# One bank of scores in eight copied by ScalarE, its maximum kept by VectorE from bf16 copies

## The reference, cut to what matters

```python
q = (query @ Wq.T + bq).reshape(b, -1, 16, 16)      # 256 latent tokens
k = (key @ Wk.T + bk).reshape(b, -1, 16, 16)        # 4096 context tokens
v = (value @ Wv.T + bv).reshape(b, -1, 16, 16)
attn = softmax(einsum('bqhd,bkhd->bhqk', q, k) / sqrt(16))
out = einsum('bhqk,bkhd->bqhd', attn, v) ; out @ Wo.T + bo
```

## Time and profile before

| | us |
|---|---|
| median of 3 runs | 3688.89 (3686.14 to 3690.83) |
| span of the profiled execution, first to last instruction | 3677.2 |
| outside the span: median less span | 11.7 |
| DVE busy in the whole span | 2126.4 (58%) |
| ACT busy in the whole span | 1525.3 (41%) |

### The profile page before, as it was taken

How to read it: one execution, slowest core, us unless ns; L and a number is a source line. 1 busy time by engine, 2 the same in 40 slices (tenths; PEclk the granted TensorE clock), 3 DMA queues, 4 the chain that set the end, 5 groups by cost and what they waited for, 6 DMA issues and landing times. The chain is left out here.

```text
span 3677.2 us, 56678 instructions
## 1 busy us (share of the span) xinstructions
PE 3396.7 (92%) x22589; PEld 2130.7 (58%) x22608; DVE 2126.4 (58%) x3378; ACT 1525.3 (41%) x2294; POOL 904.2 (25%) x665
## 2 busy tenths in 40 slices
PE   8989898999999999999967888999988889999899
PEld 5855695655656556565634576444455644445575
DVE  4335313555555555555468621999855279995654
ACT  2335211424334243343355522466745137665621
POOL 1032001426345163452517512000011120000430
PEclk9999999999999999999988999999999989999999
DMA  5358562000000100000097533756500386550010
GB/s 190 105 188 273 186 249 84 7 6 5 7 1 1 61 7 9 4 4 1 12 241 281 206 143 120 190 117 121 101 26 24 124 226 125 117 106 22 1 48 36
DMA packets 228860, 346.91 MB, mean 94 GB/s; under 512 B 104176, under 2 KB 177584, under 8 KB 223984
## 3 DMA queue, kind: packets, MB, share of 16 engines
q1 hardware_dynamic: 228208, 342.16, 32.1%
q0 software_dynamic: 384, 1.05, 0.1%
HBM read 257.15 MB, written 86.02 MB: 93 GB/s over the span
## 5 line engine op out<-in xcount | busy, mean ns | idle before, releaser
L1421 POOL TENSOR_TENSOR L1x_acc<-L1x_acc,L1x_pr 128x512 f32<-128x512 f32 x256 | 418.0, 1633 | 135.7 <-ACT L1x_pr L1605 117.4
L1605 ACT ACTIVATE L1x_pr<-L1x_pss 128x1024 f32<-128x1024 f32 x272 | 278.4, 1024 | 288.2 <-PE L1x_pss L1515 280.5
L1651 DVE TENSOR_TENSOR L1x_acc<-L1x_acc,L1x_pr 128x512 f32<-128x512 f32 x256 | 255.4, 997 | 213.2 <-ACT L1x_pr L1605 209.4
L1234 DVE TENSOR_REDUCE L3x_pk<-L3x_psm 128x1 f32<-128x512 f32 x512 | 328.8, 685 | 25.9 <-PE L3x_psm L1063 19.4
L1234 DVE TENSOR_REDUCE L2x_pk<-L2x_psm 128x1 f32<-128x512 f32 x512 | 328.8, 685 | 20.7 <-PE L2x_psm L1063 14.1
L1211 ACT ACTIVATE L3x_pr<-L3x_pss 128x1024 f32<-128x1024 f32 x256 | 248.1, 1021 | 106.3 <-PE L3x_pss L1106 106.0
L1211 ACT ACTIVATE L2x_pr<-L2x_pss 128x1024 f32<-128x1024 f32 x256 | 248.1, 1021 | 102.0 <-PE L2x_pss L1106 101.8
L1629 DVE TENSOR_REDUCE L1x_pk<-L1x_psm 128x2 f32<-128x1024 f32 x144 | 168.0, 1167 | 211.1 <-PE L1x_psm L1453 211.1
L1515 PE MATMUL L1x_pss<-L1x_Q,L1x_K 64*128 64x256 f32 x2176 | 279.3, 376 | 0.0
L1479 PE MATMUL L1x_pss<-L1x_w,L1x_cT 128*128 128x256 f32 x1088 | 257.5, 387 | 0.0
L1474 PE MATMUL L1x_pss<-L1x_cT,L1x_w 128*128 128x512 f32 (+1 forms) x576 | 256.4, 584 | 0.5 <-DMA L1x_cT<-normed_context 0.5
(11 more groups left out here) (742 smaller groups left out, 6126.7 us busy)
## 6 DMA issues: line engine op xcount, KB each, us to landing
f0e_wt<-in_f_pieces SPq DMA_DIRECT2D x10, 3072.0 KB, 11.5
offset_rows<-s_rows SPq DMA_DIRECT2D x32, 768.0 KB, 5.8
L2x_KS<-L2x_key_parts SPq DMA_DIRECT2D x24, 1024.0 KB, 12.8
L3x_KS<-L3x_key_parts SPq DMA_DIRECT2D x24, 1024.0 KB, 12.8
s_add<-offset_rows SPq DMA_DIRECT2D x32, 512.0 KB, 7.5
n_cT<-in_ctxT SPq DMA_DIRECT2D x32, 512.0 KB, 4.6
f1e_wt<-in_f_pieces SPq DMA_DIRECT2D x8, 2048.0 KB, 12.7
L2x_key_parts<-n_kst SPq DMA_DIRECT2D x32, 384.0 KB, 2.8
```

The source lines that it names most:

```text
L1234: nc.vector.reduce_max(pk[:, n % 2, h * QT + qt, j:j + 1], psm[:, x % 3, :], AX).then_inc(turn_read, 1)
L1421: i = nc.gpsimd.tensor_tensor(acc[:, n, 1, :, :], acc[:, n, 1, :, :], pr[:, A % RING, :, 1, :], ALU.add)
L1605: nc.scalar.activation(pr[:, A % RING, :, :, :].rearrange("p h e q -> p (h e q)"), pss[:, x:x + 2, :].rearrange("p h n -> p (h n)"), ACT.E ...
L1651: i = nc.vector.tensor_tensor(acc[:, n, 0, :, :], acc[:, n, 0, :, :], pr[:, A % RING, :, 0, :], ALU.add)
```

## The change

In every unit from 1 on, the products i = 7, 15, ..., 55 (the second of their pair, all of query tile 1 of the group's last head, key chunks 0 to 6) are no longer read by DVE from PSUM. ACT copies the bank to SBUF as bf16 (into `most` for i = 7, into one of two buffers `side` for the others), and DVE takes the elementwise maximum of `most` and the copy. Number 63 is still read as before. When it is read, DVE reduces the 7 other columns of `mx`, then `most` (128 x 512 bf16) to one column, waits for that, and makes the last column of `mx` by a third reduce over two numbers. The copies stand in ACT's queue behind the second exponential of a pair of slots. PE's `claim` waits for whichever engine reads the bank. The buffers lie in `qp`, which is not used in the loop.

```diff
+    ASIDE = NJ - 1
+        side, most = qp[:, 0, :, :], qp[:, 1, :, :]
+        def beside(n, i):
+            return n >= 1 and i % 8 == 7 and i // 8 < ASIDE
+        def beside_before(n, i):
+            return ASIDE * (n - 1) + i // 8
...
-            def claim():
+            def claim(side_copy=None):
                 x = taken[0]
                 taken[0] += 1
                 if x >= 3:
-                    pe.wait_ge(turn_read, x - 2)
+                    pe.wait_ge(*readers[x - 3])
+                if side_copy is None:
+                    by_dve[0] += 1
+                readers.append((turn_read, by_dve[0]) if side_copy is None else (aside, side_copy + 1))
                 return x
...
+            def copy_beside(n, first, last):
+                for i in range(first, last):
+                    if beside(n, i):
+                        c = beside_before(n, i)
+                        act.wait_ge(turn, turns[n, i] + 1)
+                        if i < 8 and n >= 3:
+                            act.wait_ge(peak, n - 1)
+                        elif i >= 24:
+                            act.wait_ge(aside_read, c - n - 1)
+                        into = most[:, n % 2, :] if i < 8 else side[:, c % 2, :]
+                        nc.scalar.copy(into, psm[:, turns[n, i] % 3, :]).then_inc(aside, 1)
+            act.wait_ge(scratch_out, 16 * KC)
+            act.wait_ge(sel_mm, 2 * NU)
+            copy_beside(1, 0, AHEAD)
             for a in range(UNITS * STEPS):
...
+                if a % 2:
+                    for x in (a % STEPS - 1, a % STEPS):
+                        copy_beside(*of_slot(a // STEPS, x))
...
             def read_peaks(n, first, last):
                 for i in range(first, last):
                     x = written()
+                    if beside(n, i):
+                        c = beside_before(n, i)
+                        if i >= 8:
+                            dve.wait_ge(aside, c + 1)
+                            if i >= 16:
+                                dve.wait_ge(aside_read, c - n)
+                            nc.vector.tensor_tensor(most[:, n % 2, :], most[:, n % 2, :], side[:, c % 2, :], ALU.max).then_inc(aside_read, 1)
+                        continue
                     nc.vector.reduce_max(pk[:, n % 2, h * QT + qt, j:j + 1], psm[:, x % 3, :], AX).then_inc(turn_read, 1)
...
+                    elif i == NP - 1:
+                        dve.wait_ge(turn_read, reads[0])
+                        nc.vector.reduce_max(mx[:, n % 2, 0:UH * QT - 1], pk[:, n % 2, 0:UH * QT - 1, :], AX)
+                        dve.wait_ge(aside_read, (ASIDE - 1) * n)
+                        link(nc.vector.reduce_max(pk[:, n % 2, UH * QT - 1, 0:1], most[:, n % 2, :], AX))
+                        nc.vector.reduce_max(mx[:, n % 2, UH * QT - 1:UH * QT], pk[:, n % 2, UH * QT - 1, 0::NJ - 1], AX).then_inc(peak, 1)
```

More of the change, by code:

```diff
@@ L922, in narrow_attention @@
     ONE = len(KPART) * hd
+    ASIDE = NJ - 1
     names = ("w_here wv_here q_mm q_act part1 part2 sel_mm sel_in masked masked_more scratch_out qs_in kh_in0 kh_in1 ks_in0 ks_in1 v_in0 v_in1 cleared ones_rows ones_in "
-             "c_here0 c_here1 c_here2 c_here3 v_mm v_ev v_out0 v_out1 v_out2 turn turn_read peak scored exps averaged o_copied chain").split()
+             "c_here0 c_here1 c_here2 c_here3 v_mm v_ev v_out0 v_out1 v_out2 turn turn_read aside aside_read peak scored exps averaged o_copied chain").split()
     with Tensors(nc) as u, stage(nc, *[pre + "_" + n for n in names]) as (block, *sems):
         (w_here, wv_here, q_mm, q_act, part1, part2, sel_mm, sel_in, masked, masked_more, scratch_out, qs_in, kh_in0, kh_in1, ks_in0, ks_in1, v_in0, v_in1, cleared,
-         ones_rows, ones_in, c_here0, c_here1, c_here2, c_here3, v_mm, v_ev, v_out0, v_out1, v_out2, turn, turn_read, peak, scored, exps, averaged, o_copied, chain) = sems
+         ones_rows, ones_in, c_here0, c_here1, c_here2, c_here3, v_mm, v_ev, v_out0, v_out1, v_out2, turn, turn_read, aside, aside_read, peak, scored, exps, averaged, o_copied, chain) = sems
         kh_in, ks_in, v_in, c_here, v_outs = (kh_in0, kh_in1), (ks_in0, ks_in1), (v_in0, v_in1), (c_here0, c_here1, c_here2, c_here3), (v_out0, v_out1, v_out2)
@@ L966, in of_slot @@
             return (m, i, i + NP // SLOTS) if m < UNITS else (m, 0, 0)
+        def beside(n, i):
+            return n >= 1 and i % 8 == 7 and i // 8 < ASIDE
+        turns = {}
+        def beside_before(n, i):
+            return ASIDE * (n - 1) + i // 8
         @block.sync
@@ L1040, in _ @@
             taken = [0]
+            by_dve, readers = [0], []
             rows_out = {}
-            def claim():
+            def claim(side_copy=None):
                 x = taken[0]
@@ L1061, in products @@
                     j, qt, h = peak_of(i)
-                    for r, x in enumerate((claim(), claim())):
+                    for r, x in enumerate((claim(), claim(beside_before(n, i + 1) if beside(n, i + 1) else None))):
+                        turns[n, i + r] = x
                         nc.tensor.matmul(psm[:, x % 3, :], QM[64 * r:64 * r + 64, y, h, b * S + qt * P:b * S + (qt + 1) * P],
@@ L1086, in rows @@
                     i.then_inc(turn, 1)
-                rows_out[n] = taken[0]
+                rows_out[n] = by_dve[0]
             def denominators(n):
@@ L1212, in _ @@
                                      pss[:, 2 * (a % 2):2 * (a % 2) + 2, :].rearrange("p x q -> p (x q)"), ACT.Exp, scale=SCALE).then_inc(exps, 1)
+                if a % 2:
+                    for x in (a % STEPS - 1, a % STEPS):
+                        copy_beside(*of_slot(a // STEPS, x))
         @block.vector
         def _(dve):
-            links, taken = [0], [0]
+            links, taken, reads = [0], [0], [0]
             def link(i):
@@ L1233, in read_peaks @@
                     x = written()
+                    if beside(n, i):
[6 more added lines that the diff above has]
+                        continue
+                    reads[0] += 1
                     nc.vector.reduce_max(pk[:, n % 2, h * QT + qt, j:j + 1], psm[:, x % 3, :], AX).then_inc(turn_read, 1)
-                    if i == NP - 1:
-                        dve.wait_ge(turn_read, x + 1)
+                    if i == NP - 1 and n == 0:
+                        dve.wait_ge(turn_read, reads[0])
                         nc.vector.reduce_max(mx[:, n % 2, :], pk[:, n % 2, :, :], AX).then_inc(peak, 1)
+                    elif i == NP - 1:
+                        dve.wait_ge(turn_read, reads[0])
+                        nc.vector.reduce_max(mx[:, n % 2, 0:UH * QT - 1], pk[:, n % 2, 0:UH * QT - 1, :], AX)
+                        dve.wait_ge(aside_read, (ASIDE - 1) * n)
+                        link(nc.vector.reduce_max(pk[:, n % 2, UH * QT - 1, 0:1], most[:, n % 2, :], AX))
+                        nc.vector.reduce_max(mx[:, n % 2, UH * QT - 1:UH * QT], pk[:, n % 2, UH * QT - 1:UH * QT, 0::NJ - 1], AX).then_inc(peak, 1)
             def take_rows(n):
```

## The result

The changed kernel takes 3697.63 us (median of 13 runs) against 3684.07 for the kernel before on the same chips. The ratio is 1.0033, with a 95% interval of 1.0024 to 1.0042, that is 12.2 us (8.8 to 15.5). It leaves out one slow run of the changed kernel, of 3859.95 us with a granted clock of 0.922 where the others have 0.967 to 0.974. The profiled execution has a span of 3690.3 us, 13.1 more than the one before.

A forecast was written before the change was run, and what follows sets the result against it. PE's own spacing of 1.305 us a slot was taken to bound the loop, not DVE. 12 closings at 0.79 add 9.5 us: 3677.2 + 9.5 of span, with 11.7 around it, make 3698.4 us; range 3682 to 3706.

The forecast's parts named there:

- the 9.5: Total added over both blocks: 12 closings with products behind them, at 0.79 us each; forecast chance 0.54.
- the term of 11.7 us: Time around the profiled span of 3677.2 us that the median implies, the median taken as that execution's time.
- What bounds: In the loop, PE's own spacing of 1.305 us a slot, with 0.04 a slot of slack in the first-bank ring.
- three views of the profile: DVE's costliest groups, its busy 15.46 of 15.68 us, and PEld's 208 waits for it (72.9 us): "DVE bounds the loop".
- Reads removed, worth 0: 7 second-bank reads a unit at 0.61, 4.27 us of DVE, lie outside the ring of first-bank reads: no gain.
- Elementwise maxima: 6 a unit on DVE in place of a second-bank read: 0.35 us each to the next start, nothing moves.
- The dear end of 0.3 more each: Case of elementwise maxima at the 997 ns of another block: 0.3 us more each, 6 a unit, kept for the range.
- Copies: 49 a block on ACT behind odd slots' products, 585 ns each, exponentials held 0.03 at worst: cost 0.
- The closing: In slot 25, three reduces before the next first-bank read: 0.93 us against 0.14, +0.79 each, 6 a block.
- the signs to look for: In the changed profile: pairs 1.305 apart, DVE near 14 of 15.7, 2.2 after a closing, each block 4.7 us longer.

The follow-up runs named there:

- e2: Changed kernel with the 7 banks a unit read by nobody, no copies or elementwise maxima, one closing reduce; 1.0010 of the kernel before.
- e4: Changed kernel plus a needless DVE reduce of 256 f32 behind each of 84 elementwise maxima; 1.0036 of the kernel before.
- e5: Changed kernel plus 84 needless DVE reduces of 256 f32 behind second-bank reads where nothing is taken aside; 1.0055 of the kernel before.
- e1: Changed kernel without its two extra closing reduces, copies and elementwise maxima kept; 1.0004 of the kernel before.
- e6: Changed kernel with a needless second ACT copy behind each of the 98 copies; 1.0059 of the kernel before.
- v2_folded: Changed kernel with banks i = 5, 13, ..., 53 aside, kept maximum folded to 256 wide, reduced in slot 20, one closing reduce; 1.0208 of the kernel before.
- e3: Changed kernel with the closing's reduce of the kept maxima done twice, each waited for; 1.0058 of the kernel before.
- e7: Changed kernel with the reduce of the kept maxima moved from slot 25 to slot 21, no third reduce; 1.0017 of the kernel before.
- v4: v2_folded with the banks taken aside put back to i = 7, 15, ..., 55, in odd slots; 1.0019 of the kernel before.

## Why the prediction was right

*The number.* 3698.4 us were predicted and 3697.63 measured, and that closeness is in part luck. The prediction added 9.5 us to a median of 3688.89 from 3 runs; 13 runs of the same kernel have a median of 3684.07, 4.8 lower. Against that base the change cost 13.6 us between the medians, 12.2 by the ratio, and not 9.5. The two errors nearly cancel. What is to be judged is the 9.5 (the interval is 8.8 to 15.5) and its terms. Nor is the term of 11.7 us what it was taken for: in every run whose profiled execution has its time on record, time less span is 1.8 us, so by that some 9.9 of the 11.7 lay inside it: the profiled execution of the kernel before was faster than the median. The sum does not depend on this, as it only adds the 9.5 to the median.

*What bounds.* This was right, and against three views of the profile. DVE's share, its groups and PEld's waits for it all pointed to DVE; PE's starts, with the same 0.98 in a unit without products, said that they were not stretched. The plainest answer is e2: DVE at 38.32 of 43.37 us (88%) in the place of 42.76 (99%), unit unchanged. The spacings of e4 and e5 say the same: equal work of DVE costs 0.10 a unit in one place and 1.07 in another. What the Trainium skill ("Perfetto Trace Analysis", Identifying the Most-Contended Engine) would have one do, take the engine of the highest occupancy, fails here by e2's number: the occupancy was real, the bound was not.

*Reads removed, worth 0.* Right: the pairs behind a copy stay at 1.31, but for the one of slot 31, 0.02 late. The prediction had no term for it: it had not asked when the read behind a skipped bank starts.

*Elementwise maxima.* 0.35 to the next start was taken, 424 ns long, as the 256 f32 elements. The profile has 42 a block at 0.424. The dear end of 0.3 more each, which the prediction says its range keeps, would have been 25 us over 14 units and is not in 3682 to 3706; the 0.424 made that of no account. The Trainium skill's rule ("VectorE: DVE Perf Modes", The perf-mode tier table) holds in both halves, bf16 in SBUF at twice the rate for the elementwise form, and none for the reduce: 676 ns for 512 bf16 elements from SBUF, where 512 f32 took 686.

*Copies.* 585 ns and no cost were predicted. The profile has 49 a block of 586 ns; e1 puts copies and maxima together at 0.02 us a unit, and by e6 some 0.41 us of cover were left.

*The closing.* Predicted term by term 0.13, 0.69 + 0.04 and 0.07, less 0.14: 0.79. Measured 0.12, 0.71 and 0.08, less 0.14: 0.77, and 0.775 in the spacing of PE's pairs. 12 times, with unit 7's closing free (DVE is still idle for 1.2 before its rows): 9.3 us of the 12.2. Besides it an undisturbed unit is longer by 0.03, nearly all of it the pair of slot 31; over 14 units that is some 0.4. The rest, about 2.5 us, lies within the interval (8.8 to 15.5), and I assign it to nothing: outside the closings the two profiles differ by single PE stalls of 1 to 3 us that come and go (one of 2.23 us before a weight load of L2x, with no releaser, is in the profile before and not in the one after), and by 4.7 us that were there before L2x began.

*What was off in the signs to look for.* I had DVE near 14 of 15.7 us in twelve slots; it is 14.99 of 15.72. Only three of the twelve slots have an elementwise maximum, and each leaves DVE idle for 0.17: 3 x 0.17 on top of the 0.22 (15.68 less 15.46) that it was idle before. And 4.7 us more in each block came out, from the first product to the last denominators, as 3.1 and 6.5, with those stalls in it; their sum, 9.6, is beside the 9.5 predicted, but single stalls alone move such a sum by 2 us and more.

## What to carry to other kernels

Ask of an engine that is busy all the time whether it stretches the starts of the engine that waits for it: compare their spacing with a stretch in which that engine has nothing to wait for. In a ring of buffers with an order written by hand, price every edit by the one read that the ring waits for; work moved off the others is worth nothing, and what is gathered at one point to pay for it lands on that read in full. Here that was 0.77 us at each of 12 closings, and nothing for 4.44 us of reads in a unit. A helper's queue counts too: the same copy was free behind two exponentials that had ended, and cost about 1 us each time behind two that had not (6.1 us a unit for 6 of them in v2_folded).

## What the runs showed of the hardware

In the kernel before two reduces of DVE on 512 elements start 0.61 apart though each is 0.68 long; in e5 one of 256 (0.41 long) leaves 0.33 to the next start. In the changed kernel an ACT exponential of 1.02 us starts 0.51 after a copy that is 0.59 long. A read's end to PE's next pair was 0.15 us wherever PE was waiting for that read, in the kernel before, in the changed one and in e3, e5, e7, v2 and v4. The end of a product to the DVE read that waited for it was 0.04, also behind idle times of over 1 us in the kernel before; it was 0.11 behind a bank that DVE skips with nothing in its place (slot 30 of the changed kernel, and the banks left out in e2). What makes that difference no run shows.
